# Layer 0 cross attention: four score-maxima banks, three score banks, and exponentials by head

## The chip, the cores and the metric

The kernel runs on one core of one Trainium2 chip. The metric is device time in microseconds (us) for one execution of the whole two-layer decoder. The core has a matmul engine (TensorE, PE in the profile; its weight loads are PEld), a vector engine (VectorE, DVE), an activation engine (ScalarE, ACT), a general engine (GpSimd, POOL) and SyncE (SP), which issues most transfers. Each engine runs its own instructions in program order; semaphores tie the engines together. Matmuls write into PSUM, which has eight banks of 512 float32 per partition. ACT and DVE read them.

## What is computed

Two decoder layers, each of self attention, cross attention and a feed-forward part with a layer norm after each. The change is in the cross attention of layer 0: 8 x 56 = 448 queries against all 8 x 1500 = 12000 keys, 16 heads of 16 dimensions, with fake quantisation of q, k, v and of the attention weights.

```python
q = _fq_sym(q, axis=-1)
k = _fq_sym(k, axis=-1)
v = _fq_sym(v, axis=2)
attn = jnp.einsum('bhqd,bhkd->bhqk', q, k)
attn = jax.nn.softmax(attn.astype(jnp.float32), axis=-1)
attn = _fq_unsigned(attn, axis=-1)
out = jnp.einsum('bhqk,bhkd->bhqd', attn, v)
```

`_fq_unsigned` scales a row by its own maximum over 255, so the largest weight of a row becomes 255. For this the kernel needs the maximum of every row of scores before it rounds, and so it goes over the scores twice.

## The kernel before, in words

The cross attention of layer 0 (`layer0_cross_attention`) works on pairs of heads, 8 pairs. The two heads of a pair lie in different halves of the partitions (rows 0 to 63 and 64 to 127 of the PE array). For each pair there are two passes over the 12000 keys.

- **First pass.** Blocks of 500 keys, 24 blocks to a pair. A matmul (lines 855 and 874) gives a 128 x 500 tile of scores for 128 queries of a head, and DVE takes its row maximum (`highest`, line 1094). The 2 x 448 queries of a pair make 7 such tiles to a block: "pair" 0 (P0, two tiles, one of each head), "one" 0, "pair" 2 (P2, two tiles), "mixed" (M, the rest of both heads) and "one" 1. The tiles go through a ring of three banks (`ring(n)`, line 580). `ring_free(n)` (line 842) lets PE write tile n once DVE has taken tile n - 3, counted by the semaphore `taken`; `given` tells DVE that a tile is there.
- **Second pass.** Tiles of 125 keys, 96 to a pair, 4 to a block. `score(n)` (line 913) makes the scores of both heads of a tile, two matmuls of 448 queries (line 923) into two banks. The four banks 4 to 7 hold two tiles. ACT takes the exponential of both heads in one instruction of 125 x 896 (line 1283); POOL rounds it (line 777); PE multiplies two tiles of it with the values and sums it (`product`, lines 935 and 940, into bank 3). A product works on tiles from four before. `score(n)` waits for `exp` n - 1, that is until the tile two before has been read.
- **Side work.** The keys and values of layer 1's cross attention are projected in between (`side`, lines 904 and 908, float32), through the same ring.

Both passes run at once, the second a pair and two blocks behind the first. The order of PE's work in a block T is a table, `ORDER` (line 437), read by `steps(T)` (line 465), which PE and DVE both go through. T runs from 0 to 217: from 0 to 191 there is a first pass, from 26 to 217 a second. A "side" piece comes behind the first free place of `SIDE_PLACES`, which is behind P0 where a block has one piece. By `side_halves` (line 446), of the 166 blocks with both passes (T = 26 to 191) 78 have no side piece and 88 have one; 24 of the last 26 blocks, which have the second pass alone, have one too. In this document these are the **plain blocks**, the **side blocks** and the **tail**. The four scores of a block are s0 to s3, the two products V0 and V1. In a plain block PE's order was s0, s1, P0, V0, one 0, P2, s2, s3, M, V1, one 1.

At a change of pair (T % 24 == 1), PE makes a "maxima" tile behind P0 from what DVE has cut (`cut_maxima`); line 884 waits for it.

Of the kernel before, what the change touches and what calls it, by code (L numbers as in the profile page):

```python
# [13 lines left out]
ACT = mybir.ActivationFunctionType  # L14
# [3 lines left out]
TOKENS = B * T  # L18
# [4 lines left out]
KP = 125  # L23
# [5 lines left out]
LN255 = float(np.log(255.0))  # L29
# [16 lines left out]
UNSCALE = 1.0 / (SPLIT_SCALE * SPLIT_SCALE)  # L46
ROUND_AT = 1024.0
K_PARTS = (0, 1, None, 0)
Q_PARTS = (0, 0, None, 1)
MAX_ROW = 32  # L50


class Core:
# [367 lines left out]
def load_keys(sp, k, pair, chunk):  # L421

    at = slice(chunk * CHUNK, (chunk + 1) * CHUNK)
    for side in range(2):
        h = 2 * pair + side
        for j, part in enumerate(K_PARTS):
# [7 lines left out]
SIDE_FROM, SIDE_EARLY, SIDE_LATE = 4, 20, 6  # L434
SIDE_MID = 4 * (UNITS - SIDE_EARLY - SIDE_LATE)
SIDE_PLACES = ("pair", 0), ("one", 0), ("score", 3), ("one", 1)
ORDER = (("score", 0), ("score", 1), ("pair", 0), ("product", 0), ("one", 0), ("pair", 2), ("score", 2), ("score", 3),
         ("mixed", 0), ("product", 1), ("one", 1))


def second(T):

    return T - (BLOCKS + LAG)
# [51 lines left out]
def layer0_cross_attention(nc, k, d):  # L495

    with ExitStack() as ctx:
        sb = lambda n, sh, dt=F32: ctx.enter_context(nc.sbuf_tensor(n, sh, dt))
        SLOTS = 6
# [3 lines left out]
        kx = k.kx  # L503
# [42 lines left out]
        expo = late(KP, 0, 5376).rearrange("p (s a n) -> p s a n", s=SLOTS, a=2)  # L546
# [10 lines left out]
        bias = k.sum_all[0:TP, 2 * D:3 * D]  # L557
# [5 lines left out]
        ps = ctx.enter_context(nc.psum_tensor("c0_ps", [128, 8, 512], F32))  # L563
# [3 lines left out]
        s = k.sems("c0", "side_w side_l0 side_l1 side_st0 side_st1 side_ones qx qx_zero q_mixed kx_ones w const "  # L567
                   "given taken rows link scored2 exp rounded vlink pv pv_sb tail ctx ctxT ctxT_sb y "
                   + NORM_SEMS)
# [7 lines left out]
        y = ps[0:TP, 2:4, :].rearrange("p b (t n) -> p (b t) n", n=D)  # L577
        pv = ps[:, 3, 0:TOKENS]
        place = ring_places()
        ring = lambda n: ps[:, n % 3, :]  # L580
        wide = HD + 1

        def rounds(engine, step, flush=lambda r: None, after={}):
# [24 lines left out]
        with nc.Block() as block:  # L608

            @block.sync  # L610
            def _(sp):
# [6 lines left out]
                def max_rows_of_ones(slot):  # L618
                    for side in range(2):
                        row = 64 * side + MAX_ROW  # L620
                        sp.dma_start(kx[row:row + 16, slot, :].rearrange("p (b n) -> p b n", n=BLOCK),
# [98 lines left out]
            def _(pool):  # L720
# [23 lines left out]
                for i in range(4):  # L744
                    pool.wait_ge(s["const"], i + 1)
                    of = slice((i % 2) * wide, (i % 2 + 1) * wide)
# [26 lines left out]
                sum_values(KT // 16 - 1)  # L773

                for n in range(PAIRS * KT):
                    pool.wait_ge(s["exp"], n + 1)
                    nc.gpsimd.tensor_scalar(probs[:, n % SLOTS], expo[:, n % SLOTS], ROUND_AT, 1.0,  # L777
                                            ALU.add, ALU.mult).then_inc(s["rounded"], 1)

            @block.tensor  # L780
            def _(pe):
# [58 lines left out]


                def ring_free(n):
                    if n >= 3:
                        pe.wait_ge(s["taken"], n - 2)

                def keys_loaded(T):
                    pair, at = divmod(T, BLOCKS)
# [30 lines left out]
                def maxima(pair):  # L878
# [4 lines left out]
                    for t in range(3):  # L883
                        nc.tensor.matmul(ring(n)[MAX_ROW:MAX_ROW + 3, t * 128:(t + 1) * 128],
                                         row_parts[:, pair % 2, t, :], k.ident_h[:], start=True, stop=True)
                        nc.tensor.matmul(ring(n)[64 + MAX_ROW:64 + MAX_ROW + 3, 64 + t * 128:64 + (t + 1) * 128],
                                         row_parts[:, pair % 2, 4 + t, :], k.ident_h[:], start=True, stop=True)
                    nc.tensor.matmul(ring(n)[MAX_ROW:MAX_ROW + 3, 384:448], row_parts[:, pair % 2, 3, :],
                                     k.ident_h[:, 0:64], start=True, stop=True)
                    nc.tensor.matmul(ring(n)[64 + MAX_ROW:64 + MAX_ROW + 3, 0:64], row_parts[:, pair % 2, 3, :],  # L890
                                     k.ident_h[:, 64:128], start=True, stop=True).then_inc(s["given"], 1)
# [21 lines left out]
                def score(n):  # L913

                    pair, tile = divmod(n, KT)
                    if tile == 0:
                        pe.wait_ge(s["taken"], place["maxima", pair] + 1)
                    if n >= 2:
                        pe.wait_ge(s["exp"], n - 1)
                    keys = slice(tile * KP, (tile + 1) * KP)  # L920
                    for a in range(2):
                        of = slice(64 * a, 64 * a + 64)
                        last = nc.tensor.matmul(ps[0:KP, 4 + 2 * (n % 2) + a, 0:TOKENS], kx[of, pair % 2, keys],  # L923
                                                qx[of, pair, :], start=True, stop=True)
                    last.then_inc(s["scored2"], 1)

# [44 lines left out]
                for T in range(TIMES):  # L971
# [6 lines left out]
                    n = second(T) * TILES_PER_BLOCK  # L978
# [26 lines left out]
                for t in range(TT):  # L1005
                    for c in range(C2):
                        last = nc.tensor.matmul(y[:, t, :], ctx_T[:, c, t * TP:(t + 1) * TP], w[:, c, :],
                                                start=(c == 0), stop=(c == C2 - 1))
# [204 lines left out]
            def _(act):  # L1213
# [65 lines left out]
                for n in range(PAIRS * KT):  # L1279
                    act.wait_ge(s["scored2"], n + 1)  # L1280
                    if n >= SLOTS:
                        act.wait_ge(s["pv"], (n - SLOTS) // 2 + 1)
                    nc.scalar.activation(expo[:, n % SLOTS], ps[0:KP, 4 + 2 * (n % 2):6 + 2 * (n % 2), 0:TOKENS],  # L1283
                                         ACT.Exp, scale=UNSCALE, bias=LN255).then_inc(s["exp"], 1)
                    if n % KT == 3 and n > KT:
                        take_groups(n // KT - 1)
                take_groups(PAIRS - 1)
# [836 lines left out]
```

## Time and profile before

| what | value |
| --- | --- |
| runs, device us | 2118.14 median of 3 (2116.51 to 2120.32) |
| the profiled execution | 2118.8 us, its span 2116.8 us |
| mean granted TensorE clock | 0.929 of full speed |
| PE busy | 1850.5 us (87%) |
| DVE busy | 1388.2 us (66%) |
| ACT busy | 1100.3 us (52%) |
| POOL busy | 968.3 us (46%) |

The span runs from the first to the last instruction of the profiled execution; the device time has about 2 us more around it. A share of busy time is a mean over stages with different limits, so the stretch that the change touches has to be read by itself. A line of the timeline merges neighbouring instructions of one kind: its length runs from the first start to the last end, and the bracket gives the idle time before it and the instruction that ended it. Matmuls are pipelined: one starts before the one ahead of it has ended, and the ends are modelled.

### The profile page before, as it was taken

The page shows a single profiled execution, that of the slowest core. Times are in us where ns is not written, and L with a number is a line of the kernel's source. Part 1 is how long each engine was busy: PE and PEld are TensorE (multiplying, and loading weights), DVE is VectorE, ACT ScalarE, POOL GpSimd, SP SyncE. Part 2 cuts the span into 40 slices and gives each one's busy share as a digit, 9 for nine tenths or more (in the row PEclk, how much of TensorE's full clock was granted, in tenths as well). Part 3 has the DMA queues.
Part 4 walks back from the last instruction along what each step waited for, and adds up shares of the span by engine and source line. Part 5 has one row for each costly group of instructions (what it writes and reads, how often), then busy time and mean ns, then how long its engine had stood idle before and what let it go on. Part 6 is the DMA issues. An engine that isn't in the chain of part 4 may idle for free. (4 is left out here: it accounts for less than half of the span.)

```text
span 2116.8 us, 38630 instructions
## 1 busy us (share of the span) xinstructions
PE 1850.5 (87%) x15222; PEld 984.8 (47%) x15222; DVE 1388.2 (66%) x2437; ACT 1100.3 (52%) x1573; POOL 968.3 (46%) x1021
## 2 busy tenths in 40 slices
PE   7986999869989999999999999999996594888678
PEld 3575888634433333333333333333332393666444
DVE  1444777759988888888888888888211352565522
ACT  2251566544256666666666656666774252555411
POOL 1001455469556667666667767677784100000000
PEclk9997999869989999999999999999998656899889
DMA  5002444674411221211112111100110103543000
GB/s 206 1 1 60 116 121 117 141 119 125 124 37 32 45 48 27 43 42 33 42 27 48 38 32 40 43 24 16 41 41 11 58 1 97 200 145 130 19 1 9
DMA packets 103179, 132.20 MB, mean 62 GB/s; under 512 B 8879, under 2 KB 94707, under 8 KB 102644
## 3 DMA queue, kind: packets, MB, share of 16 engines
q1 hardware_dynamic: 102148, 128.39, 22.9%
q8 instruction: 114, 1.87, 0.4%
q10 hardware_dynamic: 864, 1.51, 0.2%
q14 instruction: 53, 0.43, 0.1%
HBM read 89.78 MB, written 38.55 MB: 61 GB/s over the span
## 5 line engine op out<-in xcount | busy, mean ns | idle before, releaser
L1094 DVE TENSOR_REDUCE c_top<-c_ps 128x1 f32<-128x500 f32 x1344 | 827.4, 670 | 122.5 <-PE c_ps L855 97.6
L777 POOL TENSOR_SCALAR c_values<-c_values 125x896 f16<-125x896 f32 x768 | 719.7, 937 | 334.0 <-ACT c_values L1283 301.1
L1283 ACT ACTIVATE c_values<-c_ps 125x896 f32<-125x896 f32 x768 | 660.7, 915 | 352.2 <-PE c_ps L923 351.8
L935 PE MATMUL c_ps<-c_values,c_total 125*32 125x448 f32 x3072 | 369.3, 552 | 1.5 <-POOL c_values L777 1.5
L855 PE MATMUL c_ps<-kx,c_qx 64*128 64x500 f16 x1152 | 305.5, 387 | 21.1 <-DVE c_top L1094 11.1
L923 PE MATMUL c_ps<-c_qx,kx 64*125 64x448 f16 x1536 | 269.8, 362 | 4.1 <-ACT c_values L1283 3.9
L855 PEld LDWEIGHTS c_ps<-kx,c_qx 64*128 64x128 f16 x1152 | 76.0, 93 | 267.0 <-DVE c_top L1094 176.6
L797 PE MATMUL c_ps<-shared_w,c_rows 128*125 128x256 f32 x768 | 186.4, 386 | 0.0
L1775 DVE TENSOR_SCALAR c_clipped<-c_ps 125x896 f32<-125x896 f32 x96 | 104.0, 1089 | 89.8 <-PE c_ps L1690 88.1
L797 PEld LDWEIGHTS c_ps<-shared_w,c_rows 128*125 128x125 f32 x768 | 147.6, 192 | 25.1 <-issue 0.4
L1926 POOL MEMSET f_select<- 8x1408 f32 x1 | 1.3, 1261 | 335.6 <-POOLq L66 335.6
L923 PEld LDWEIGHTS c_ps<-c_qx,kx 64*125 64x125 f16 x1536 | 122.5, 135 | 63.7 <-ACT c_values L1283 25.3
L1743 ACT ACTIVATE c_probs<-c_clipped,c_attend 125x896 f32<-125x896 f32 x96 | 108.0, 1133 | 80.8 <-DVE c_clipped L1775 80.8
L1690 PE MATMUL c_ps<-c_qheads,c_kT 64*125 64x224 f32 x768 | 109.9, 405 | 44.0 <-DMA c_v<-v 41.2
L940 PE MATMUL c_ps<-c_values 125*16 125x448 f16 x1536 | 143.5, 353 | 0.0
L904 PE MATMUL c_ps<-c_rows,shared_w 128*128 128x250 f32 x384 | 110.8, 412 | 27.8 <-DMA c_rows<-in_ctx_T 15.0
L908 PE MATMUL c_ps<-shared_w,c_rows 128*125 128x256 f32 x384 | 110.3, 411 | 12.2 <-DVE c_top L1094 7.5
L935 PEld LDWEIGHTS c_ps<-c_values,c_total 125*32 125x32 f32 x3072 | 60.7, 108 | 114.6 <-issue 103.1
L1690 PEld LDWEIGHTS c_ps<-c_qheads,c_kT 64*125 64x125 f32 x768 | 72.5, 200 | 55.7 <-issue 24.4
L904 PEld LDWEIGHTS c_ps<-c_rows,shared_w 128*128 128x128 f32 x384 | 68.2, 198 | 64.7 <-issue 25.2
L725 POOL TENSOR_TENSOR c_kback<-c_kback,c_kscale 125x512 f32<-125x512 f32 x48 | 51.8, 1080 | 93.1 <-ACT c_kback L1223 93.1
L874 PE MATMUL c_ps<-kx,x_T 128*128 128x500 f16 x192 | 75.1, 391 | 21.2 <-DVE c_top L1094 17.4
(274 smaller groups left out, 2089.4 us busy)
## 6 DMA issues: line engine op xcount, KB each, us to landing
c_rows<-in_ctx_T SPq DMA_DIRECT2D x96, 250.0 KB, 5.3
kx<-k_parts SPq DMA_DIRECT2D x192, 93.8 KB, 3.8
v<-c_halves SPq DMA_DIRECT2D x48, 265.6 KB
c_v<-v SPq DMA_DIRECT2D x8, 1593.8 KB
k_parts<-c_parts SPq DMA_DIRECT2D x48, 250.0 KB, 2.6
k_T<-c_kback SPq DMA_DIRECT2D x48, 250.0 KB
c_kT<-k_T SPq DMA_DIRECT2D x8, 1500.0 KB
f_wgu<-in_f_Wgu SPq DMA_DIRECT2D x2, 1408.0 KB, 10.5
```

Source lines behind the costliest of these rows:

```text
L777: nc.gpsimd.tensor_scalar(probs[:, n % SLOTS], expo[:, n % SLOTS], ROUND_AT, 1.0, ALU.add, ALU.mult).then_inc(s["rounded"], 1)
L797: last = nc.tensor.matmul(bank[:, j * D:(j + 1) * D], rows[:, u % 3, c, j * KP:(j + 1) * KP], kv_w[:, c, of], start=False, stop=(c == C2 - 1),
L855: nc.tensor.matmul(ring(n)[:, 0:BLOCK], qx[of, pair, q0:q0 + 128], kx[of, pair % 2, at * BLOCK:(at + 1) * BLOCK], start=True, stop=True).t ...
L904: last = nc.tensor.matmul(ring(n)[:, 0:UNIT], side_w[:, 0, c, half * 128:(half + 1) * 128], rows[:, a, c, :], start=(c == 0), stop=(c == C ...
L908: last = nc.tensor.matmul(ring(n)[0:KP, 0:D], rows[:, a, c, half * KP:(half + 1) * KP], side_w[:, 1, c, :], start=(c == 0), stop=(c == C2 ...
L923: last = nc.tensor.matmul(ps[0:KP, 4 + 2 * (n % 2) + a, 0:TOKENS], kx[of, pair % 2, keys], qx[of, pair, :], start=True, stop=True)
L935: nc.tensor.matmul(ps[32 * g:32 * g + 32, 3, 0:TOKENS], total[:], expo[:, n % SLOTS, g % 2, :], start=(at == 0), stop=False, skip_group_ch ...
L940: last = nc.tensor.matmul(ps[32 * g:32 * g + HD, 3, 0:TOKENS], v_steps[:, n % KT, h * HD:(h + 1) * HD], probs[:, n % SLOTS, g % 2, :], sta ...
L1094: nc.vector.tensor_reduce(top[:, pair % 2, tile, at:at + 1], ring(n)[:, 0:BLOCK], AX.X, ALU.max)\
L1283: nc.scalar.activation(expo[:, n % SLOTS], ps[0:KP, 4 + 2 * (n % 2):6 + 2 * (n % 2), 0:TOKENS], ACT.Exp, scale=UNSCALE, bias=LN255).then_i ...
L1690: last = nc.tensor.matmul(ps[0:KP, 2 + 2 * (i % 2) + a, c * 4 * T:(c + 1) * 4 * T].rearrange("p (h t) -> p h t", h=4), k_T[of, parity, c, ...
L1743: nc.scalar.activation(probs[:, i % 3], clipped[:, i % 2], ACT.Exp, scale=attend[:, 0, at], bias=attend[:, 1, at]).then_inc(s["exp"], 1)
```

## The change

The first pass gets a ring of four banks (0, 1, 2 and 5) and the second pass three score banks (4, 6, 7), one to a head, in turn. `score(n)` writes the halves 2n and 2n + 1 of that turn, and waits for `exp` 2n - 1, that is until the first head of the tile before has been read. ACT takes the exponential of each head by itself, 125 x 448, with a count of `exp` for each; POOL waits for both. In `ORDER`, P0 comes between s0 and s1, and P2 between s2 and s3.

```diff
@@ -48,6 +48,7 @@
+RING, SCORES = (0, 1, 2, 5), (4, 6, 7)
@@ -434,7 +435,7 @@
-ORDER = (("score", 0), ("score", 1), ("pair", 0), ("product", 0), ("one", 0), ("pair", 2), ("score", 2), ("score", 3),
+ORDER = (("score", 0), ("pair", 0), ("score", 1), ("product", 0), ("one", 0), ("score", 2), ("pair", 2), ("score", 3),
          ("mixed", 0), ("product", 1), ("one", 1))
@@ -577,7 +578,8 @@
-        ring = lambda n: ps[:, n % 3, :]
+        ring = lambda n: ps[:, RING[n % len(RING)], :]
+        score_bank = lambda i: ps[0:KP, SCORES[i % len(SCORES)], 0:TOKENS]
@@ -773,7 +775,7 @@
-                    pool.wait_ge(s["exp"], n + 1)
+                    pool.wait_ge(s["exp"], 2 * n + 2)
@@ -840,8 +842,8 @@
                 def ring_free(n):
-                    if n >= 3:
-                        pe.wait_ge(s["taken"], n - 2)
+                    if n >= len(RING):
+                        pe.wait_ge(s["taken"], n - len(RING) + 1)
@@ -915,12 +917,12 @@
-                    if n >= 2:
-                        pe.wait_ge(s["exp"], n - 1)
+                    if n >= 1:
+                        pe.wait_ge(s["exp"], 2 * n + 2 - len(SCORES))
                     keys = slice(tile * KP, (tile + 1) * KP)
                     for a in range(2):
                         of = slice(64 * a, 64 * a + 64)
-                        last = nc.tensor.matmul(ps[0:KP, 4 + 2 * (n % 2) + a, 0:TOKENS], kx[of, pair % 2, keys],
+                        last = nc.tensor.matmul(score_bank(2 * n + a), kx[of, pair % 2, keys],
                                                 qx[of, pair, :], start=True, stop=True)
                     last.then_inc(s["scored2"], 1)
@@ -1280,8 +1282,9 @@
-                    nc.scalar.activation(expo[:, n % SLOTS], ps[0:KP, 4 + 2 * (n % 2):6 + 2 * (n % 2), 0:TOKENS],
-                                         ACT.Exp, scale=UNSCALE, bias=LN255).then_inc(s["exp"], 1)
+                    for a in range(2):
+                        nc.scalar.activation(expo[:, n % SLOTS, a], score_bank(2 * n + a), ACT.Exp,
+                                             scale=UNSCALE, bias=LN255).then_inc(s["exp"], 1)
```

**A plain block on PE**, its first half, from one 1 of the block before to one 0. L855 (L857 in the changed kernel) are first-pass tiles, L923 (L925) score matmuls, L935 and L940 (L937 and L942) the product. Before:

```order
L855 MATMUL c_ps<-kx,c_qx 128x500 [waits c0_taken]
L923 MATMUL c_ps<-c_qx,kx 125x448 [waits c0_exp,kx_loaded02]
L923 MATMUL c_ps<-c_qx,kx 125x448
L923 MATMUL c_ps<-c_qx,kx 125x448 [waits c0_exp]
L923 MATMUL c_ps<-c_qx,kx 125x448
L855 MATMUL c_ps<-kx,c_qx 128x500 [waits c0_taken]
L855 MATMUL c_ps<-kx,c_qx 128x500
L935 MATMUL c_ps<-c_values,c_total 32x448 [waits c0_rounded]
L935 MATMUL c_ps<-c_values,c_total 32x448 x3
L940 MATMUL c_ps<-c_values 16x448 x4
L855 MATMUL c_ps<-kx,c_qx 128x500 [waits c0_taken] x2
```

And now:

```order
L857 MATMUL c_ps<-kx,c_qx 128x500 [waits c0_taken]
L925 MATMUL c_ps<-c_qx,kx 125x448 [waits c0_exp,kx_loaded02]
L925 MATMUL c_ps<-c_qx,kx 125x448
L857 MATMUL c_ps<-kx,c_qx 128x500 [waits c0_taken]
L857 MATMUL c_ps<-kx,c_qx 128x500
L925 MATMUL c_ps<-c_qx,kx 125x448 [waits c0_exp]
L925 MATMUL c_ps<-c_qx,kx 125x448
L937 MATMUL c_ps<-c_values,c_total 32x448 [waits c0_rounded]
L937 MATMUL c_ps<-c_values,c_total 32x448 x3
L942 MATMUL c_ps<-c_values 16x448 x4
L857 MATMUL c_ps<-kx,c_qx 128x500 [waits c0_taken]
L925 MATMUL c_ps<-c_qx,kx 125x448 [waits c0_exp]
```

The two matmuls of P0 now stand between s0 and s1, and s1 waits for `exp` with one pair of tiles ahead of it on PE; the product V0 stands behind that wait. Behind one 0 it is the score s2 that follows, where P2 stood.

**A side block on PE**, the same place. L908 (L910) is the side piece. Before:

```order
L923 MATMUL c_ps<-c_qx,kx 125x448 [waits c0_exp]
L923 MATMUL c_ps<-c_qx,kx 125x448
L923 MATMUL c_ps<-c_qx,kx 125x448 [waits c0_exp]
L923 MATMUL c_ps<-c_qx,kx 125x448
L855 MATMUL c_ps<-kx,c_qx 128x500 [waits c0_taken]
L855 MATMUL c_ps<-kx,c_qx 128x500
L908 MATMUL c_ps<-shared_w,c_rows 125x256 [waits c0_taken]
L908 MATMUL c_ps<-shared_w,c_rows 125x256
L935 MATMUL c_ps<-c_values,c_total 32x448 [waits c0_rounded]
L935 MATMUL c_ps<-c_values,c_total 32x448 x3
```

And now:

```order
L925 MATMUL c_ps<-c_qx,kx 125x448 [waits c0_exp]
L925 MATMUL c_ps<-c_qx,kx 125x448
L857 MATMUL c_ps<-kx,c_qx 128x500 [waits c0_taken]
L857 MATMUL c_ps<-kx,c_qx 128x500
L910 MATMUL c_ps<-shared_w,c_rows 125x256 [waits c0_taken]
L910 MATMUL c_ps<-shared_w,c_rows 125x256
L925 MATMUL c_ps<-c_qx,kx 125x448 [waits c0_exp]
L925 MATMUL c_ps<-c_qx,kx 125x448
L937 MATMUL c_ps<-c_values,c_total 32x448 [waits c0_rounded]
L937 MATMUL c_ps<-c_values,c_total 32x448 x3
```

P0 and the side piece now stand between s0 and s1, and s1 stands between the side piece and the product.

## Rows read from the trace of the kernel before

**Rows 1.** One line's instructions: lines 855 and 923; ns shortest/median/longest, first and last start.
```profile
L855 PE MATMUL c_ps<-kx,c_qx x1152: 367/381/619, 412.3 to 1490.5; 64*128 64x500 f16 x192
...
L923 PE MATMUL c_ps<-c_qx,kx x1536: 349/349/632, 591.6 to 1609.3; 64*125 64x448 f16 x192
```

**Rows 2.** Engines by stretch: length, us busy of PE, PEld, DVE, ACT, POOL, then granted clock.
```profile
600.00:1490.00 890.00, 841.79 (x7033) 315.06 (x7036) 764.16 (x1299) 570.02 (x664) 615.81 (x658) 1.00 0.16 37
```

**Rows 3.** Timeline of DVE, two blocks: start, length, count, idle time before and what ended it.
```profile
905.16 7.17 DVE L1094 TENSOR_REDUCE c_top<-c_ps 128x1 f32<-128x500 f32 x11
...
913.76 3.23 DVE L1094 TENSOR_REDUCE c_top<-c_ps 128x1 f32<-128x500 f32 x5 [0.97 <-PE c_ps L855]
```

**Rows 4.** Timeline of PE's matmuls in the same two blocks.
```profile
905.52 0.38 PE L855 MATMUL c_ps<-kx,c_qx 64*128 64x500 f16 x1
905.52 0.76 PE L923 MATMUL c_ps<-c_qx,kx 64*125 64x448 f16 x4
905.95 0.54 PE L855 MATMUL c_ps<-kx,c_qx 64*128 64x500 f16 x2
906.42 0.96 PE L935 MATMUL c_ps<-c_values,c_total 125*32 125x448 f32 x8
...
907.50 0.73 PE L855 MATMUL c_ps<-kx,c_qx 64*128 64x500 f16 x3
908.07 0.54 PE L923 MATMUL c_ps<-c_qx,kx 64*125 64x448 f16 x4
908.66 0.39 PE L874 MATMUL c_ps<-kx,x_T 128*128 128x500 f16 x1
908.97 0.96 PE L935 MATMUL c_ps<-c_values,c_total 125*32 125x448 f32 x8
...
910.05 0.38 PE L855 MATMUL c_ps<-kx,c_qx 64*128 64x500 f16 x1
...
911.21 1.13 PE L908 MATMUL c_ps<-shared_w,c_rows 128*125 128x256 f32 x4 [0.18 <-DVE c_top L1094]
912.26 0.96 PE L935 MATMUL c_ps<-c_values,c_total 125*32 125x448 f32 x8
...
914.50 0.38 PE L874 MATMUL c_ps<-kx,x_T 128*128 128x500 f16 x1 [0.18 <-DVE c_top L1094]
...
915.90 0.38 PE L855 MATMUL c_ps<-kx,c_qx 64*128 64x500 f16 x1
```

**Rows 5.** Timeline of ACT in the first of the two blocks.
```profile
906.13 1.73 ACT L1283 ACTIVATE c_values<-c_ps 125x896 f32<-125x896 f32 x2 [0.61 <-PE c_ps L923]
908.46 1.73 ACT L1283 ACTIVATE c_values<-c_ps 125x896 f32<-125x896 f32 x2 [0.61 <-PE c_ps L923]
```

**Rows 6.** ACT's groups by form: busy us, mean ns of one.
```profile
L1283 ACT ACTIVATE c_values<-c_ps 125x896 f32<-125x896 f32 x768 | 660.7, 915 | 352.2 <-PE c_ps L923 351.8
...
L1277 ACT ACTIVATE c_values<-c_ps 128x448 f32<-128x448 f32 x8 | 4.4, 544 | 4.8 <-PE c_ps L949 4.8
```

**Rows 7.** Timeline in the tail, a block after the first pass has ended: PE's matmuls.
```profile
1529.07 0.40 PE L923 MATMUL c_ps<-c_qx,kx 64*125 64x448 f16 x2 [0.22 <-ACT c_values L1283]
...
1529.40 1.11 PE L904 MATMUL c_ps<-c_rows,shared_w 128*128 128x250 f32 x4
...
1530.44 0.96 PE L935 MATMUL c_ps<-c_values,c_total 125*32 125x448 f32 x8
...
1533.74 0.40 PE L923 MATMUL c_ps<-c_qx,kx 64*125 64x448 f16 x2 [0.22 <-ACT c_values L1283]
```

**Rows 8.** Timeline of ACT in the same block of the tail.
```profile
1531.97 1.73 ACT L1283 ACTIVATE c_values<-c_ps 125x896 f32<-125x896 f32 x2 [1.33 <-PE c_ps L923]
```

**Rows 9.** Engines by stretch, columns as above: three stretches with waits of PE.
```profile
1849.00:1869.50 20.50, 17.26 (x432) 12.96 (x436) 12.43 (x19) 12.51 (x12) 0.00 (x0) 1.00 0.45 158
1236.00:1241.50 5.50, 4.14 (x26) 1.53 (x28) 3.92 (x7) 0.86 (x2) 1.87 (x2) 0.69 0.04 10
1106.00:1110.50 4.50, 2.50 (x29) 1.02 (x29) 4.42 (x8) 1.27 (x2) 2.04 (x3) 1.00 0.00 0
```

## The prediction

> **What bounds the kernel now.** I read first where the changed code runs, then who is busy there, then two single blocks instruction by instruction.
>
> The first pass runs from 412 to 1490 us, the second from 592 to 1609 us [rows 1]. Where both run, 592 to 1490, there are 166 blocks, 78 plain and 88 with a side piece (counted from `side_halves`). In that stretch PE is busy 842 us of 890 and DVE 764, at full clock (1.00, that is 2.4 GHz) [rows 2]. Both look like the bound, and a mean cannot tell which it is, so look at a block of each kind.
>
> *Plain block*, from one head tile "one 1" at 905.52 to the next at 910.05: **4.53 us** [rows 4]. DVE runs through it without a gap: 11 maxima in 7.17 us, so one in 0.65 us, and the seven of a block take 4.55 [rows 3]. So a plain block is bound by DVE. PE's own work in it, counted by starts: from one 1 to the second tile of P0 0.60 (905.52 to 906.12, the last start of a line that is 0.54 long with matmuls of 0.37 to 0.38), 0.30 until the product, which has another shape, 1.08 for V0 (906.42 to 907.50), then one 0, P2, s2 and s3 in about 0.60 (0.2 for the first, 0.19 for each two matmuls of both heads: the scores of 908.07 and 908.26), 0.30 until M, 0.31 to V1, 1.08 for V1: **4.27 us**. PE has only 0.26 to spare.
>
> *Side block*, 910.05 to 915.90: **5.85 us** [rows 4]. DVE stands idle 0.97 in it, waiting for PE's next tile [rows 3], and PE waits 0.18 for DVE twice, ahead of the side piece and ahead of M [rows 4]. PE's own work is 4.27 + 1.05 (911.21 to 912.26) = 5.32. Here the ring of three makes the two engines wait for each other in turn.
>
> As a check: 78 x 4.53 + 88 x 5.85 = 868 us of the 898; the rest lies at the changes of pair and in longer products.
>
> **What the change removes.** A ring of four lets PE run one tile further ahead of DVE. In side blocks that can take away up to 5.85 - 5.32 = 0.53 each, 47 us in all. In plain blocks it brings nothing as long as DVE sets their length.
>
> **What the change adds: a wait of PE for ACT.** With three score banks, s1 may not start until ACT has read the first head of s0, and s3 not until it has read the first head of s2. What that takes, from rows:
> - From the start of a score to the start of its exponential: s0 905.52 to 906.13, 0.61 (its second head starts behind one 1, which sits in the same half of the array); s2 908.07 to 908.46, 0.39 [rows 4, 5].
> - An exponential of 448. The trace has none. ACT's 896 take 915 ns and its copy of 448 takes 544 [rows 6]; the difference of 371 ns for 448 columns gives 0.83 ns a column and 0.17 fixed, so 0.54. It cannot be under 0.37, the columns alone, nor near 0.915. I take 0.54, the row of the same size.
> - From ACT's end to PE's next start: in the tail, ACT ends at 1531.97 + 1.73 = 1533.70 and a score starts at 1533.74, 0.04 to 0.05 [rows 7, 8].
>
> So s1 comes no earlier than 0.61 + 0.54 + 0.05 = 1.20 after s0, and s3 0.39 + 0.54 + 0.05 = 0.98 after s2. What the new order puts between is P0 and P2, 0.19 of PE time each. Everything behind the score in PE's queue (V0 and one 0; M, V1 and one 1) waits with it, and DVE waits for the tiles among these.
>
> *Plain block, new chain* (from one 1): s1 at 1.20; V0 at 1.50 (change of shape, 0.30); one 0 at 2.58; s2 at 2.78; s3 at 3.76; M at 4.06; V1 at 4.37; next one 1 at 5.45. Against 4.53 that is +0.92; s0 waits for s3's first head, which is done 1.0 after s3, while PE needs 1.69: no wait there. DVE needs 4.55 and now idles; with four banks it holds PE up nowhere. 78 x 0.92 = **+72**.
>
> *Side block, new chain*: P0's second tile at 0.41 (the 0.60 above less the 0.19 of s1), the side piece at 0.71, s1 behind it at 1.76, by when ACT has long read s0: the side piece hides the whole first wait. V0 at 2.06, one 0 at 3.14, then as in a plain block 2.87 to the next one 1: 6.01. Against 5.85 that is +0.16, with the 0.53 of removed waits already in it: the second wait (0.6) and one more change of shape (side piece to s1 to V0, about 0.1) eat them. 88 x 0.16 = **+14**.
>
> *Tail*, 26 blocks from 1490, 4.67 each (1529.07 to 1533.74) [rows 7]: side piece behind s0, so s1 waits for nothing; s2 to s3 has no P2 between, 0.98 instead of 0.19. From s0: side piece 0.30, s1 1.34, V0 1.64, s2 2.72, s3 3.70, V1 4.00, next s0 5.08: 0.41 x 24 = +10, and the last two blocks, without side piece, about +1.1 each: **+12**.
>
> *Changes of pair*: PE waits there for DVE's cut maxima behind P0, the place where s1 now waits too. The two waits lie side by side, so 0.6 is counted too much at 7 places: **-4**.
>
> At nothing: ACT's second start (two halves overlap by 0.10, as 1.73 for two exponentials of 915 shows [rows 5], so a tile occupies ACT 0.88 instead of 0.81, 3.5 us of a 5.45 block; the block's length covers it, and without that cover it would cost 0.3 a block); POOL's wait for both halves (0.07 later, products are four tiles behind); blocks before T = 26, which have no second pass and which DVE bounds. No transfer moves.
>
> **Sum**: 72 + 14 + 12 - 4 = +94 on the profiled execution's 2118.8 us (span 2116.8): **2213 us**. The median of the runs is 2118.1, so nothing shifts.
>
> *Ends.* Low: s1 follows 0.39 rather than 0.61 behind s0, as s3 does behind s2 (-17); side blocks end no longer than before (-14); changes of pair hide more (-6); exponentials start earlier by what the model of matmul ends leaves open, 0.1 a wait (-20): 2156. High: the 0.36 of PE's waits for DVE in a side block stays (+32), and an exponential takes 0.05 longer in 270 waits (two in a plain block, one in the others, +13): 2258.
>
> The Trainium skill ("ScalarE: Activation LUTs", section "What ACT_TABLE_LOAD costs") gives an ACTIVATE 186 ns and 0.833 ns a column, and 93 ns more for a bias given by pointer. An estimate from it is 0.65 for such a half, so 0.11 more for each of the 270 waits left, which would make the sum 2243. The row speaks against the pointer: 915 ns for 896 columns is below even the page's 932 without one.
>
> **Rivals.**
> 1. *Faster.* The fourth ring bank decides and the exponentials by head are quick enough to hide. Then plain blocks stay at DVE's 4.53 and side blocks fall to PE's 5.32: -47, **2072**. For it: DVE's 0.97 of idle time in a side block is real. Against it: both waits together would have to fit into 0.26 of spare PE time in a plain block, and the start of ACT behind a score alone takes 0.39. It decides only if s1 can follow s0 within about 0.55. 9%.
> 2. *Nothing.* The gains in side blocks balance the waits in plain ones: 0.5 a plain block (+39), side blocks at PE's 5.32 (-47), the tail +10: 2121, within 0.2%. It needs every term at its own end. 2%.
> 3. *The clock falls.* With two more pauses of PE in a block, the granted clock could drop to 1.2 GHz. From 1236 to 1241.5, with PE busy 4.14 of 5.50, it is 0.69 in the mean; from 1106 to 1110.5, with PE busy 2.50 of 4.50, it is 1.00, and from 1849 to 1869.5, busy 17.3 of 20.5, it is 1.00 as well [rows 9]. The new plain block has PE busy about 4.6 of 5.45, as that last stretch. One block in ten at half clock (4.27 more each, 19 of 192) is +81: **2294**. The Trainium skill ("TensorE: Matmul & The Clock Gate", section "A second HAM failure mode: psum-queue depth-cycling") tells of kernels whose short pauses between banks made the clock oscillate; by it this would be the likeliest case. The rows at 1106 and 1849 do not bear it out here. 5%.
> 4. *Half of it.* The change does less than it says: only the second wait bites, because P0 meets a wait for DVE anyway: 78 x 0.3 + 14 + 12, about **2168**, inside the range. 6%.
>
> **Numbers.** Forecast 78%, of which nearly all lies in 2156 to 2258. I take 2155 to 2260; it holds rival 4 too and leaves out the others, some 18% with the forecast's own edges. Faster by over 0.2% (about what a measurement of this kernel can tell): 9%; within: 2%; slower: 89%.
>
> **What would show it.** Right: plain blocks of about 5.45 us; PE idle ahead of s1 and s3, ended by ACT, some 0.4 each; ACT's halves at 0.54; DVE idle about 0.9 a plain block, waiting for PE; side blocks near 6.0, with no PE wait for DVE. Wrong: plain blocks still at 4.53 with DVE gapless, or side blocks near 5.3.

## The result, and the profile after

The changed kernel takes **2216.8 us** (median of 4 runs, 2215.0 to 2218.4) against 2119.2 for the kernel before on the same chip: a ratio of 1.046, 95% interval 1.0442 to 1.0478. It is slower by 4.6%. The forecast was 2213 us, slower.

The profiled execution has a span of 2216.3 us, 99.5 more than before. Where they went is read first from the starts of the two passes. Instructions by line, lines 857 and 925 of the changed kernel (ns shortest/median/longest, first and last start), which answer to [rows 1]:

```profile
L857 PE MATMUL c_ps<-kx,c_qx x1152: 371/371/619, 409.5 to 1573.3; 64*128 64x500 f16 x192
...
L925 PE MATMUL c_ps<-c_qx,kx x1536: 349/399/632, 578.8 to 1710.1; 64*125 64x448 f16 x192
```

From these and [rows 1] the cross attention falls into three stages: the first pass alone (from the first start of its matmuls to that of the scores), both passes, and the tail (from the last first-pass matmul to the last score).

| us | first pass alone | both passes | tail |
| --- | --- | --- | --- |
| before | 179.4 | 898.9 | 118.8 |
| changed | 169.3 | 994.6 | 136.8 |
| difference | -10.1 | +95.7 | +18.0 |

That is 103.6 of loss; the first pass starts 2.8 earlier, and what follows the tail is 1.3 shorter.

With both passes, PE and DVE are both less busy than in [rows 2], at the same full clock (busy us by stretch, columns as there):

```profile
600.00:1490.00 890.00, 793.06 (x6362) 270.25 (x6362) 683.26 (x1182) 585.54 (x1198) 557.54 (x596) 1.00 0.16 34
```

The two blocks that answer to [rows 4] are here a plain one, 904.90 to 910.47, and a side block, 910.47 to 916.58. PE's timeline:

```profile
904.90 0.38 PE L857 MATMUL c_ps<-kx,c_qx 64*128 64x500 f16 x1
904.90 0.57 PE L925 MATMUL c_ps<-c_qx,kx 64*125 64x448 f16 x2
905.14 0.54 PE L857 MATMUL c_ps<-kx,c_qx 64*128 64x500 f16 x2
906.11 0.40 PE L925 MATMUL c_ps<-c_qx,kx 64*125 64x448 f16 x2 [0.42 <-ACT c_values L1286]
906.44 0.96 PE L937 MATMUL c_ps<-c_values,c_total 125*32 125x448 f32 x8
...
907.52 0.38 PE L857 MATMUL c_ps<-kx,c_qx 64*128 64x500 f16 x1
907.53 0.57 PE L925 MATMUL c_ps<-c_qx,kx 64*125 64x448 f16 x2
907.77 0.54 PE L857 MATMUL c_ps<-kx,c_qx 64*128 64x500 f16 x2
908.73 0.40 PE L925 MATMUL c_ps<-c_qx,kx 64*125 64x448 f16 x2 [0.43 <-ACT c_values L1286]
909.07 0.39 PE L876 MATMUL c_ps<-kx,x_T 128*128 128x500 f16 x1
909.38 0.96 PE L937 MATMUL c_ps<-c_values,c_total 125*32 125x448 f32 x8
...
910.47 0.38 PE L857 MATMUL c_ps<-kx,c_qx 64*128 64x500 f16 x1
...
911.18 1.11 PE L906 MATMUL c_ps<-c_rows,shared_w 128*128 128x250 f32 x4
912.22 0.40 PE L925 MATMUL c_ps<-c_qx,kx 64*125 64x448 f16 x2
912.55 0.96 PE L937 MATMUL c_ps<-c_values,c_total 125*32 125x448 f32 x8
...
914.85 0.40 PE L925 MATMUL c_ps<-c_qx,kx 64*125 64x448 f16 x2 [0.43 <-ACT c_values L1286]
...
916.58 0.38 PE L857 MATMUL c_ps<-kx,c_qx 64*128 64x500 f16 x1
```

A plain block is 5.57 us long (4.53 before), the side block 6.11 (5.85). In the plain block PE stands idle 0.42 and 0.43 us, at 906.11 (s1) and 908.73 (s3), each time for ACT. In the side block the piece at 911.18 starts without a wait, and so does s1 behind it at 912.22; only s3 at 914.85 waits. ACT and then DVE in the same plain block:

```profile
908.14 2.02 ACT L1286 ACTIVATE c_values<-c_ps 125x448 f32<-125x448 f32 x4 [0.61 <-PE c_ps L925]
```

```profile
905.32 1.85 DVE L1096 TENSOR_REDUCE c_top<-c_ps 128x1 f32<-128x500 f32 x3 [0.51 <-PE c_ps L857]
907.94 2.44 DVE L1096 TENSOR_REDUCE c_top<-c_ps 128x1 f32<-128x500 f32 x4 [0.77 <-PE c_ps L857]
```

ACT runs two tiles by halves in 2.02 us and then waits for PE; DVE, which went on without a break in [rows 3], waits 0.51 and 0.77 us for PE's next tile. The page's costliest groups say the same of the whole run (busy us, mean ns of one | idle time before, and what ended it):

```profile
L1286 ACT ACTIVATE c_values<-c_ps 125x448 f32<-125x448 f32 x1536 | 751.2, 541 | 371.9 <-PE c_ps L925 355.1
...
L925 PE MATMUL c_ps<-c_qx,kx 64*125 64x448 f16 x1536 | 364.5, 391 | 122.3 <-ACT c_values L1286 122.3
...
L857 PE MATMUL c_ps<-kx,c_qx 64*128 64x500 f16 x1152 | 305.1, 384 | 10.4 <-DVE x_T L1089 5.8
```

PE's matmuls of line 925 have 122.3 us of idle time ahead of them, all ended by ACT. Summed by place from the trace, 32.9 of it lie ahead of s1 and 71.3 ahead of s3 while both passes run, and 17.9 in the tail: that is 0.42 us for each of the 78 plain blocks and 0.43 for each of all 166. An exponential of 448 columns takes 541 ns.

### The profile page after: what moved, and what is told of

Its sections match the earlier page's. It is cut to its first block and busy times, and to the rows that moved or that the text cites. A ratio compares the mean times of both kernels' runs of the same rounds, so it can differ in the third digit from the quotient of the medians.

```text
span 2216.3 us, 39398 instructions
## 1 busy us (share of the span) xinstructions
PE 1883.2 (85%) x15222; PEld 967.0 (44%) x15222; DVE 1370.9 (62%) x2437; ACT 1190.8 (54%) x2341; POOL 968.3 (44%) x1021
## 5 line engine op out<-in xcount | busy, mean ns | idle before, releaser
L1286 ACT ACTIVATE c_values<-c_ps 125x448 f32<-125x448 f32 x1536 | 751.2, 541 | 371.9 <-PE c_ps L925 355.1
L925 PE MATMUL c_ps<-c_qx,kx 64*125 64x448 f16 x1536 | 364.5, 391 | 122.3 <-ACT c_values L1286 122.3
L937 PE MATMUL c_ps<-c_values,c_total 125*32 125x448 f32 x3072 | 368.6, 552 | 0.1
L857 PE MATMUL c_ps<-kx,c_qx 64*128 64x500 f16 x1152 | 305.1, 384 | 10.4 <-DVE x_T L1089 5.8
L925 PEld LDWEIGHTS c_ps<-c_qx,kx 64*125 64x125 f16 x1536 | 105.7, 132 | 307.8 <-ACT c_values L1286 303.8
L857 PEld LDWEIGHTS c_ps<-kx,c_qx 64*128 64x128 f16 x1152 | 92.5, 108 | 252.2 <-DVE c_top L1096 164.5
L942 PE MATMUL c_ps<-c_values 125*16 125x448 f16 x1536 | 143.0, 352 | 0.0
L910 PE MATMUL c_ps<-shared_w,c_rows 128*125 128x256 f32 x384 | 110.1, 410 | 0.1
L937 PEld LDWEIGHTS c_ps<-c_values,c_total 125*32 125x32 f32 x3072 | 60.6, 108 | 81.4 <-issue 80.7
L1152 DVE TENSOR_SCALAR c_kback<-c_ps,c_sidebk 128x250 f32<-128x250 f32 x96 | 45.5, 474 | 71.2 <-PE c_ps L906 70.9
```

Source lines behind the costliest of these rows:

```text
L857: nc.tensor.matmul(ring(n)[:, 0:BLOCK], qx[of, pair, q0:q0 + 128], kx[of, pair % 2, at * BLOCK:(at + 1) * BLOCK], start=True, stop=True).t ...
L910: last = nc.tensor.matmul(ring(n)[0:KP, 0:D], rows[:, a, c, half * KP:(half + 1) * KP], side_w[:, 1, c, :], start=(c == 0), stop=(c == C2 ...
L925: last = nc.tensor.matmul(score_bank(2 * n + a), kx[of, pair % 2, keys], qx[of, pair, :], start=True, stop=True)
L937: nc.tensor.matmul(ps[32 * g:32 * g + 32, 3, 0:TOKENS], total[:], expo[:, n % SLOTS, g % 2, :], start=(at == 0), stop=False, skip_group_ch ...
L942: last = nc.tensor.matmul(ps[32 * g:32 * g + HD, 3, 0:TOKENS], v_steps[:, n % KT, h * HD:(h + 1) * HD], probs[:, n % SLOTS, g % 2, :], sta ...
L1286: nc.scalar.activation(expo[:, n % SLOTS, a], score_bank(2 * n + a), ACT.Exp, scale=UNSCALE, bias=LN255).then_inc(s["exp"], 1)
```

## The experiments

Each is told with its edit against the kernel before or the changed one. "Plain", "side" and "tail" are medians over the blocks of a kind, taken from one start of M to the next (in the tail, of s0). Stages are cut as above. All runs are compared with the kernel before, run on the same chips in between (2120.7 to 2120.9 us).

| kernel | us, ratio (95%) | alone | both | tail | plain | side | tail block |
| --- | --- | --- | --- | --- | --- | --- | --- |
| before | 2119.2 | 179.4 | 898.9 | 118.8 | 4.53 | 5.85 | 4.68 |
| changed | 2216.8, 1.046 | 169.3 | 994.6 | 136.8 | 5.56 | 6.13 | 5.26 |
| order alone | 2143.3, 1.012 (1.0088 to 1.0151) | 180.2 | 927.6 | 113.9 | 4.53 | 6.18 | 4.40 |
| heads alone | 2125.0, 1.0016 (1.0001 to 1.0032) | 181.6 | 899.9 | 122.0 | 4.53 | 5.85 | 4.80 |
| three banks alone | 2375.2, 1.121 (1.1192 to 1.1225) | 179.2 | 1123.6 | 153.9 | 6.12 | 7.04 | 5.96 |
| changed, old order | 2348.3, 1.108 (1.1049 to 1.1108) | 167.8 | 1104.8 | 154.0 | 5.98 | 7.04 | 5.96 |
| changed, ring of three | 2267.3, 1.070 (1.0668 to 1.0724) | 179.5 | 1032.3 | 136.9 | 5.56 | 6.57 | 5.26 |
| half exponentials | 2177.5, 1.028 (1.0254 to 1.0298) | 167.7 | 961.7 | 131.6 | 5.19 | 5.94 | 5.07 |
| spread | 2181.6, 1.029 (1.0262 to 1.0308) | 173.3 | 955.0 | 133.5 | 4.92 | 6.05 | 5.17 |
| early ring | 2109.6, 0.995 (0.9932 to 0.9971) | 168.4 | 899.0 | 118.9 | 4.53 | 5.87 | 4.68 |
| early ring, side piece behind M | 2110.6, 0.995 (0.9935 to 0.9972) | 168.6 | 899.8 | 121.5 | 4.53 | 5.90 | 4.69 |
| early ring, late order | 2099.0, 0.990 (0.9887 to 0.9918) | 168.6 | 899.1 | 113.9 | 4.53 | 5.84 | 4.40 |

**Order alone**: the kernel before with the new `ORDER`.

```diff
-ORDER = (("score", 0), ("score", 1), ("pair", 0), ("product", 0), ("one", 0), ("pair", 2), ("score", 2), ("score", 3),
+ORDER = (("score", 0), ("pair", 0), ("score", 1), ("product", 0), ("one", 0), ("score", 2), ("pair", 2), ("score", 3),
```

> The kernel before with the new order of PE's work alone (ring of three, four score banks, one exponential for both heads). If the loss comes from PE's wait for ACT with three score banks, it is not here: s1 still has two tiles of banks, and s2 goes into the 0.25 us that PE waits for DVE ahead of P2. Expected 2095 to 2120 us, plain blocks 4.3 to 4.53 us. If the order itself were the loss, about 2215 us.

The time, 2143.3 us, is above the expected range. Plain blocks stay at 4.53 us, so the order costs them nothing. But side blocks are 0.33 longer, which was not expected; that is 29 us over 88 blocks. PE's timeline of one:

```profile
909.96 0.54 PE L855 MATMUL c_ps<-kx,c_qx 64*128 64x500 f16 x2
910.87 1.13 PE L908 MATMUL c_ps<-shared_w,c_rows 128*125 128x256 f32 x4 [0.37 <-DVE c_top L1094]
911.93 0.40 PE L923 MATMUL c_ps<-c_qx,kx 64*125 64x448 f16 x2
912.26 0.96 PE L935 MATMUL c_ps<-c_values,c_total 125*32 125x448 f32 x8
```

P0 is earlier, but the side piece then waits 0.37 for DVE instead of 0.18, so nothing comes of it; and s1, now between the side piece and the product, takes 0.33 (911.93 to 912.26) where two scores in a row take 0.19 each and run into P0. A score between two other shapes takes about 0.33 here. The tail gains 4.9 us. With four score banks, then, the order alone costs 23 us; the greater loss of the change is not here.

**Heads alone**: the changed kernel with the old order, a ring of three and four score banks.

```diff
-RING, SCORES = (0, 1, 2, 5), (4, 6, 7)
+RING, SCORES = (0, 1, 2), (4, 5, 6, 7)
...
```

(The other line of the edit puts `ORDER` back.)

> Exponentials by head alone, with the old order, a ring of three and four score banks, each head's bank written again when ACT has read it (a score waits for the tile two before, as in the kernel before). If the wait with three banks is the loss, splitting the exponential costs next to nothing: 2115 to 2126 us. If ACT's second start, or POOL's later one, is the loss, 2150 to 2215 us.

It takes 2125.0 us, as expected: splitting the exponential costs about 4 us, 3.2 of them in the tail. ACT's second start is not the loss.

**Three banks alone**: the same with `SCORES = (4, 6, 7)`.

> Three score banks with exponentials by head, and nothing else: the old order and a ring of three. It closes the row of steps from the kernel before (2120) by heads alone (2125) to the changed kernel. PE waits 1.0 to 1.2 us between two scores that stand next to each other, with nothing between: plain blocks 5.98 as with the ring of four and the old order, since DVE idles there. In side blocks a ring of three may cost another 0.4 us ahead of the side piece, as it did with the new order (+39), or nothing, if the wait of 1.2 us for ACT, which now stands ahead of P0, gives DVE the time. The blocks ahead of the second pass lose 9.5. So 2358 us if the waits lie side by side, 2397 if they add.

It takes 2375.2 us, between the two cases. This is where the time goes: with the old order, one bank less for scores costs 250 us over heads alone. The price is that of the bank together with the place of the wait: `score(n)` waits for `exp` 2n - 1 ahead of both its matmuls, though the bank of the first one is free at 2n - 2. A wait for each head by itself was not tried. Side blocks are as long as with a ring of four (7.04): there the two waits lie side by side. Plain blocks lose 0.14 more than with four.

**The changed kernel with the old order**, so the ring of four added to the last one:

> The changed kernel with the old order, so that s1 stands right behind s0 and P0 and the side piece behind s1. If PE waits 1.0 to 1.2 us from one score to the next, nothing hides it now: plain blocks +0.6 us to 6.1 (+45), side blocks +1.0 (+92), the tail +0.8 a block (+20). Expected 2350 to 2390 us. If the wait is not what sets the length of a block, within 10 us of 2217.

It takes 2348.3 us, just under the range. PE's timeline, from s0 to s1 of a side block:

```profile
908.03 0.57 PE L925 MATMUL c_ps<-c_qx,kx 64*125 64x448 f16 x2
909.24 0.40 PE L925 MATMUL c_ps<-c_qx,kx 64*125 64x448 f16 x2 [0.64 <-ACT c_values L1286]
909.48 0.37 PE L857 MATMUL c_ps<-kx,c_qx 64*128 64x500 f16 x2
```

1.21 us from one score to the next with nothing between, 0.64 of it idle for ACT.

**The changed kernel with a ring of three**:

```diff
-RING, SCORES = (0, 1, 2, 5), (4, 6, 7)
+RING, SCORES = (0, 1, 2), (4, 6, 7)
```

> The changed kernel with a ring of three (banks 0 to 2) in place of four. It shows what the fourth ring bank is worth beside the new waits. Plain blocks, where DVE now idles, should stay at 5.56 us; side blocks should get back a wait of PE ahead of the side piece, 0.4 us each (+35), and blocks ahead of the second pass with four side pieces should go back from 5.9 to 6.4 us (+9). Expected 2250 to 2270 us. If the ring were what holds plain blocks, more than 2280; if it is worth nothing, 2217.

It takes 2267.3 us, as expected. Plain blocks stay at 5.56 to the hundredth: there the fourth bank does nothing. Side blocks take 0.44 more, in this wait of PE ahead of the side piece:

```profile
922.98 0.54 PE L857 MATMUL c_ps<-kx,c_qx 64*128 64x500 f16 x2
923.99 1.08 PE L906 MATMUL c_ps<-c_rows,shared_w 128*128 128x250 f32 x4 [0.46 <-DVE c_top L1096]
925.00 0.40 PE L925 MATMUL c_ps<-c_qx,kx 64*125 64x448 f16 x2
```

So the fourth bank does take away the wait it was reckoned to take away in side blocks (38 us), and 10 us in the first pass alone.

**Half exponentials**: the changed kernel, ACT reading 224 of 448 columns. The attention weights of the other half of the queries are left out of the computation.

```diff
-                        nc.scalar.activation(expo[:, n % SLOTS, a], score_bank(2 * n + a), ACT.Exp,
+                        nc.scalar.activation(expo[:, n % SLOTS, a, 0:224], score_bank(2 * n + a)[:, 0:224], ACT.Exp,
```

> The changed kernel with exponentials of the first 224 of 448 queries of each head; the other half of expo keeps old values, so the weights of those queries are left out of the computation. PE's matmuls, POOL and DVE do the same work. An exponential takes 0.17 + 0.83 x 0.224 = 0.36 us in place of 0.54. If PE stands at s1 and s3 until ACT has read the first head, each exposed wait shrinks by 0.18 to 0.19: plain blocks 5.56 to 5.19 (two waits), side blocks 6.12 to 5.94 and the tail 5.25 to 5.07 (one wait each), 50 us in all: 2160 to 2175 us. If the waits are DVE's or PE's own doing, within 5 us of 2217.

Plain blocks take 5.19 us, side blocks 5.94 and blocks of the tail 5.07, each as expected to the hundredth: the length of an exponential goes straight into PE's chain, twice in a plain block. The whole, 2177.5 us, is 2.5 above the expected range. PE's timeline, s2 to the next one 1:

```profile
906.59 0.56 PE L925 MATMUL c_ps<-c_qx,kx 64*125 64x448 f16 x2
906.83 0.54 PE L857 MATMUL c_ps<-kx,c_qx 64*128 64x500 f16 x2
907.61 0.40 PE L925 MATMUL c_ps<-c_qx,kx 64*125 64x448 f16 x2 [0.24 <-ACT c_values L1286]
...
909.53 0.38 PE L857 MATMUL c_ps<-kx,c_qx 64*128 64x500 f16 x1
```

0.24 of idle time ahead of s3 where 0.43 was, and over the run (group of line 925):

```profile
L925 PE MATMUL c_ps<-c_qx,kx 64*125 64x448 f16 x1536 | 366.1, 392 | 71.5 <-ACT c_values L1286 71.4
```

71.5 us of PE's idle time in place of 122.3. That is 51 less, as the term says; the run gained 39. The missing part is at the six changes of pair within the stage of both passes: their blocks take 52.7 us together in place of 40.8. PE waits there for DVE's cut maxima for 1.54 to 1.86 us where it waits 0.67 in the changed kernel, and in three of the blocks the clock fell (below).

**Spread**: the changed kernel with the product cut in two (`product` for the sums, `values` for the values) and other work behind every score.

```diff
-ORDER = (("score", 0), ("pair", 0), ("score", 1), ("product", 0), ("one", 0), ("score", 2), ("pair", 2), ("score", 3),
-         ("mixed", 0), ("product", 1), ("one", 1))
+ORDER = (("score", 0), ("product", 0), ("score", 1), ("values", 0), ("pair", 0), ("one", 0), ("score", 2),
+         ("product", 1), ("score", 3), ("values", 1), ("pair", 2), ("mixed", 0), ("one", 1))
...
```

> The changed kernel with each product cut into its two kinds of matmul, and an order in which at least 1.2 us of PE work stands behind every score: s0, V0 sums, s1, V0 values, P0, one 0, s2, V1 sums, s3, V1 values, P2, M, one 1. No score should wait for ACT any more. In return two scores stand alone between other shapes, 0.33 each as the order-only run showed in side blocks: plain blocks about 4.9 us, side blocks about 6.0, the tail 4.7: 2130 to 2165 us. If a plain block stays at 5.5, the wait was not for the time between two scores.

Plain blocks take 4.92 us and side blocks 6.05, as expected, and PE's wait for ACT is nearly gone (group of line 925):

```profile
L925 PE MATMUL c_ps<-c_qx,kx 64*125 64x448 f16 x1536 | 353.3, 393 | 10.5 <-ACT c_values L1293 10.5
```

It is 10.5 us. The whole, 2181.6 us, is above the range, for three reasons that the trace shows. The first pass alone takes 4 us more than in the changed kernel. The six blocks at changes of pair take 53.7 us in place of 40.8, three of them at a mean granted clock of 0.80 to 0.84. And in the tail P2, M and one 1 are missing, so only the values stand between s3 and the next s0, and the wait is back there:

```profile
1600.82 0.37 PE L946 MATMUL c_ps<-c_values 125*16 125x448 f16 x4
1601.53 0.40 PE L925 MATMUL c_ps<-c_qx,kx 64*125 64x448 f16 x2 [0.34 <-ACT c_values L1293]
```

The waits can be spread away, then, but at a price in changes of shape: ten in a plain block in place of five, and its 4.92 us are 0.65 over PE's own 4.27.

**Early ring**: the kernel before with four ring banks until the second pass begins.

```diff
-        ring = lambda n: ps[:, n % 3, :]
+        wide_until = place["pair", BLOCKS, 0] // 4 * 4
+        ring_bank = lambda n: (0, 1, 2, 5)[n % 4] if n < wide_until else (n - wide_until) % 3
+        ring = lambda n: ps[:, ring_bank(n), :]
...
-                    if n >= 3:
-                        pe.wait_ge(s["taken"], n - 2)
+                    room = 4 if n < wide_until else 3
+                    if n >= room:
+                        pe.wait_ge(s["taken"], n - room + 1)
```

> The kernel before with a ring of four (banks 0, 1, 2, 5) up to block 24 alone, where the second pass has not begun and bank 5 is free; from there on all as before. The changed kernel gained 9.5 us there (176.1 to 166.6 us from block 0 to block 25), the run with a ring of three gave it all back. If that gain is the ring's, it comes without any cost: 2107 to 2113 us, and the blocks from 26 on as in the kernel before (4.53 and 5.85 us). If the gain was from elsewhere, 2119.

It takes 2109.6 us, as expected: the 11 us of the first stage come alone and cost nothing, since bank 5 is free there.

**Early ring, side piece behind M**:

```diff
-        if (what, i) in SIDE_PLACES and sides:
+        if (what, i) in (SIDE_PLACES if len(side_halves(T)) > 1 else (("mixed", 0),)) and sides:
```

> The run before with the side piece of a one-piece block moved from behind P0 to behind M, which has its shape of the PE array. It asks whether the 0.5 us by which side blocks exceed PE's own 5.32 come from where the piece stands. If so, side blocks fall to 5.4 to 5.6 us: 2080 to 2100 us. If PE then waits for DVE in another place as long, 2105 to 2120.

It takes 2110.6 us, as the run before it; blocks with a piece are 5.90 long. PE waits for DVE ahead of the piece there too:

```profile
915.19 0.38 PE L877 MATMUL c_ps<-kx,x_T 128*128 128x500 f16 x1
915.86 1.08 PE L907 MATMUL c_ps<-c_rows,shared_w 128*128 128x250 f32 x4 [0.29 <-DVE c_top L1097]
```

The 0.5 us of a side block does not come from its place behind P0; where else it could go was not tried.

**Early ring, late order**: both gains of the change where they came alone, on the kernel before.

```diff
-    for what, i in ORDER:
+    for what, i in ORDER if scoring else LATE_ORDER:
```

(`LATE_ORDER` is the new order, used from block 192 on; the ring as in "early ring".)

> The kernel before with the two parts of the change that gained where they stood alone: the ring of four up to block 24 (-9.5 to -10 us there), and the new order in the tail alone, blocks 192 on, where the order-only run took 115.3 in place of 120.2 us to the last score (-5). Blocks 26 to 191 as in the kernel before. 2103 to 2108 us if the two gains add; 2110 if the tail's is hidden.

It takes 2099.0 us, less than expected and less than both kernels. First and last starts of the two passes:

```profile
L860 PE MATMUL c_ps<-kx,c_qx x1152: 368/381/619, 412.3 to 1480.0; 64*128 64x500 f16 x192
...
L928 PE MATMUL c_ps<-c_qx,kx x1536: 349/349/632, 580.9 to 1593.9; 64*125 64x448 f16 x192
```

The first pass alone takes 168.6 us and the tail 113.9: the two stages give 15.7 against the kernel before. The profiled spans differ by 18.3: the stage between is 0.2 longer, and 2.8 lie behind the last score, where neither edit acts and the runs here vary from 503.7 to 509.7 us. The medians differ by 21.8; the 3.5 beyond the spans is within what single runs of one kernel differ by.

## Why the prediction was right, and where its terms were off

The sum was +94 and the profiled span moved by +99.5. The mechanism, PE waiting for ACT ahead of s1 and s3, was right; that the total came within 6 us is partly luck, since terms were off in both directions. Term by term:

1. *The wait of PE for ACT* was the forecast, and it is shown: halving the exponentials shortened plain, side and tail blocks by one or two times the 0.18 to 0.19 that an exponential lost, and spreading the scores took the wait away. s1 follows one 1 by 1.21 us (904.90 to 906.11; 1.20 forecast), s3 follows one 0 by 1.21 (1.18 forecast).
2. *Plain blocks*: 5.56 in place of 5.45, so 1.03 and not 0.92 more. The changes of shape behind s1 and s3 took 0.33 and 0.34, not 0.30 each, and s3 comes 0.03 later than forecast. The exponential of s2 starts 0.61 after one 0 (907.53 to 908.14), near the 0.2 + 0.39 of the forecast, but s2 does not stand 0.2 behind one 0: one of its heads starts with it and the other 0.22 later (0.57 us for both, where a pair that starts together takes 0.40). Over 78 blocks the 0.11 is some 8 us.
3. *Side blocks*: 6.13 in place of 6.01. The mechanism held: the piece hides the first wait. The chain was right up to one 0 (3.16 us after one 1, 3.14 forecast); then s3 follows one 0 by 1.22, not 1.18, and M follows s3 by 0.33, not 0.30, and small parts make up the rest. Many blocks make this the added term with the largest error: +0.28 x 88 = 25 us in place of 14.
4. *Tail*: +18.0 in place of +12. A block takes 5.26 in place of 5.08: the three changes of shape behind a score take 0.33, not 0.30, and s3 follows s2 by 1.05, not 0.98. Over 24 blocks that is 4 of the 6 us.
5. *The first pass alone*, put at nothing since "DVE bounds" those blocks, gained 10.1. **This step was wrong.** I read a DVE timeline without gaps as a full engine. Before the side pieces begin, DVE's timeline of the kernel before and of the changed one (start, length, count):

```profile
418.86 3.20 DVE L1094 TENSOR_REDUCE c_top<-c_ps 128x1 f32<-128x500 f32 x5
422.48 4.38 DVE L1094 TENSOR_REDUCE c_top<-c_ps 128x1 f32<-128x500 f32 x7 [0.41 <-PE c_ps L855]
```

```profile
418.85 8.87 DVE L1096 TENSOR_REDUCE c_top<-c_ps 128x1 f32<-128x500 f32 x15
```

Seven maxima took 4.38 + 0.41 = 4.79 us with a ring of three, and with four they start 0.586 apart: (8.87 - 0.67) / 14. Maxima overlap when the next tile is ready, so among maxima of 0.67 that start 0.65 apart in the mean there are short waits, which the merged row does not show. That the ring gives the gain is shown by two runs: a ring of three loses it, the early ring alone has it. Of the 10.1 us, 2.7 lie in the first four blocks and 6.5 in the twenty blocks with four side pieces. By the same reading DVE's own seven are 4.10 us in a plain block too, under PE's 4.27, and its 4.53 would be the two engines waiting for each other in a ring of three. This part is read from timelines; with eight banks no run had four for the ring and four for the scores. It fits that DVE idles 1.28 us in the new plain block (0.51 + 0.77), not 0.9. The sum was hardly hurt, because with the new wait PE sets the length.
6. *Changes of pair*, -4: no run singles them out, but the traces show their size. The six of them within the stage of both passes were 15.1 us longer in all than the medians of their kinds, and are 5.2 longer now: -9.9. The forecast reason holds: PE's wait ahead of line 884 was 1.18 to 1.25 us and is 0.67 now. About 1.6 of the gain is the block T = 145, where the clock fell in the kernel before (below).

The errors of 2 to 4 (+25) stand against those of 5 (-10), of 6 (-6) and of what lies outside the three stages (-4), so the total lies nearer to the forecast than its terms do. A slip in the range did no harm: 0.1 less in each of its own 270 waits is 27 us, not 20.

Of the rivals, the first (the fourth ring bank decides) had much of its gain right, and its condition failed: beside the new waits a ring of four is worth 38 us in side blocks, 0.44 of the 0.53 each, but s1 follows s0 by 1.21 us and not by 0.55. With that the second, a balance of the two, falls too. The clock stayed at full speed in the stretch of the changed kernel above (1.00), so the third did not come. A half as long wait (the fourth) did not either: there are two waits in each plain block.

On the price of a half, the exponential is 541 ns as the copy's row said. The 0.65 worked out from the Trainium skill's "ScalarE: Activation LUTs" ("What ACT_TABLE_LOAD costs") for a bias by pointer is 0.11 more than was measured.

In one line, from the steps that were run: heads by themselves +4, three score banks +250, a ring of four -27, the new order -131: 2120.8 to 2216.8 us. The size of a step depends on what is already there: with the new order a ring of four is worth 50, and without the three banks the new order costs 23.

## What to carry to other kernels

A bank of PSUM that is moved from one ring to another has to be priced at both ends: count, for the ring that loses it, the time from the producer's start through the consumer's read back to the producer, and compare it with the work that the in-order engine has between two uses. Here that loop was 1.0 to 1.2 us and the engine had 0.2 in the new order (P0 or P2), except where the side piece stood. Where a resource is free in one stage only (bank 5 before the second pass began), use it in that stage: this gave back 0.5% with nothing lost.

A timeline row without gaps does not prove a full engine: compare the start-to-start time with the shortest one that the trace shows anywhere.

## What was not expected of the hardware

**The clock at changes of pair.** With half exponentials three blocks, T = 49, 145 and 169, took 10.0 to 11.2 us in place of 7.1. In the first of them PE stood 1.86 us for DVE's cut maxima, and the granted clock, 1.00 before, is 0.83 in the mean of the block. PE's timeline and the busy times of the stretch:

```profile
712.97 0.22 PE L886 MATMUL c_ps<-ident_h,c_rowparts 128*3 128x128 f16 x1 [1.86 <-DVE c_rowparts L1113]
```

```profile
708.60:718.60 10.00, 7.74 (x53) 2.52 (x51) 8.21 (x17) 2.42 (x8) 3.75 (x5) 0.83 0.00 1
```

The changed kernel stands 0.67 us at the same place, and its clock stays at 1.00 there. The kernel before stands 1.25 at T = 145, and that block has a mean clock of 0.82:

```profile
718.83 0.22 PE L886 MATMUL c_ps<-ident_h,c_rowparts 128*3 128x128 f16 x1 [0.67 <-DVE c_rowparts L1113]
```

```profile
1237.16 0.22 PE L884 MATMUL c_ps<-ident_h,c_rowparts 128*3 128x128 f16 x1 [1.25 <-DVE c_rowparts L1111]
```

```profile
1233.14:1242.63 9.49, 7.62 (x51) 2.71 (x52) 7.48 (x16) 3.37 (x5) 3.96 (x5) 0.82 0.13 29
```

The length of the pause does not settle it: the kernel before stands 1.25 at T = 49 and 169 too and keeps 1.00 there, and with half exponentials the three other changes of pair, with 1.54, keep it. What decides is open. The waits in each plain block, 0.42 and 0.43 of its 5.57 us, left the clock at 1.00 from 600 to 1490 us.

**A change of shape on PE** takes 0.1 to 0.15 us more than the next matmul of the same shape: in the plain block above 0.33 from s1 to V0 and 0.31 from M to V1, where a matmul of the same shape follows in 0.17 to 0.19. With 5 such changes in a plain block (behind s1, V0, s3, M and V1) this comes to about 0.65 us, near the 0.85 of the two waits.
